# Down products of the feed-forward part on the full array as one sum, the turned tile in halves, and new orders inside the periods

## The reference, cut

```python
xn = layernorm(x)
# attention: 16 heads of width 16, 2 groups of keys and values
q = rotate(xn @ wq + bq);  k = rotate(xn @ wk + bk);  v = xn @ wv + bv
attn = softmax(q @ k.T * scale)            # (4, 16, 1024, 1024)
a = (attn @ v) @ wo + bo
# feed-forward part, 1024 hidden units
hidden = silu(xn @ W1.T) * (xn @ W3.T)
f = fwht(hidden) @ W2.T                    # fwht: Walsh-Hadamard along the hidden axis
out = x + a + f
```

## Time and profile before

| | |
|---|---|
| Median of 3 runs | 1179.03 us (1177.75 to 1181.44) |
| The profiled execution | 1181.6 us, span of instructions 1179.8 us |
| TensorE | 1049.8 us busy (89%), mean granted clock 0.936 |
| VectorE | 783.2 us (66%), of it 619.3 in 512 reductions of the units |
| ScalarE | 704.7 us (60%), of it 552.9 in 1024 exponentials |
| GpSimd | 352.2 us (30%) |
| Down products (L1352) | 1536 matmuls of 64 rows by 256 columns, 279 ns each on average |
| Additions of the down products (L1104, L1106) | 32 x 0.42 us and 32 x 0.42 us |
| Turned tiles (L896, L1089) | 7 casts of 1.01 us and 7 remainders of 1.22 us in `xt` |

### The profile page before, as it was taken

One profiled execution on the slowest core, in us unless ns is written; L12 is line 12 of the kernel. 1 busy time (PEld: TensorE's weight loads), 2 busy tenths in 40 slices (PEclk: granted clock), 3 DMA queues, 4 the chain that ended last, 5 costly groups with the idle time before them and its releaser, 6 DMA issues.

```text
span 1179.8 us, 19333 instructions
## 1 busy us (share of the span) xinstructions
PE 1049.8 (89%) x7584; PEld 547.5 (46%) x7584; DVE 783.2 (66%) x891; ACT 704.7 (60%) x1318; POOL 352.2 (30%) x299
## 2 busy tenths in 40 slices
PE   0358899989998999989998999989999999999994
PEld 0314354544555455544555445554445344544552
DVE  4895477757776577766777577765777777687611
ACT  2204377656765477655775567754775667656771
POOL 1652523107330254106330164204440023102310
PEclk9755799989999899989999799989999999999997
DMA  8247022412314223412205123421204101410001
GB/s 222 67 150 192 21 67 68 101 59 72 89 31 88 70 82 88 94 63 75 83 13 109 54 99 89 88 69 31 73 20 101 48 24 46 95 36 6 7 17 51
DMA packets 62732, 84.27 MB, mean 71 GB/s; under 512 B 16688, under 2 KB 31920, under 8 KB 62640
## 3 DMA queue, kind: packets, MB, share of 16 engines
q1 hardware_dynamic: 59328, 78.30, 24.8%
q10 hardware_dynamic: 3312, 4.72, 1.6%
HBM read 55.18 MB, written 22.54 MB: 66 GB/s over the span
## 4 chain that ended last, share of the span: by engine, by line
PE 79%; DVE 12%; ACT 3%; issue 2%; ACTq 1%; SPq 1%; DMA 1%; POOL 0%; POOLq 0%; DVEq 0%
PE ps L1387 19%; PE ps L1339 16%; PE ps L1374 15%; PE ps L1297 13%; DVE negpart L1124 9%; PE ps L1352 7%; PE ps L1277 3%; PE ps L1307 3%; ACT work L942 2%; PE ps L1313 1%; ACTq L878 1%; DVE y L1106 1%; PE ps L1302 0%; DVE y L1104 0%; ACT osum L950 0%
## 5 line engine op out<-in xcount | busy, mean ns | idle before, releaser
L1124 DVE TENSOR_REDUCE negpart<-ps 128x2 f32<-128x1024 f32 x512 | 619.3, 1223 | 272.6 <-PE ps L1297 267.7
L942 ACT ACTIVATE work<-ps 128x512 f32<-128x512 f32 x1024 | 552.9, 605 | 266.4 <-PE ps L1374 211.0
L1297 PE MATMUL ps<-kb,qh 48*128 48x512 f32 x1024 | 257.7, 472 | 53.4 <-DVE negpart L1124 27.4
L1374 PE MATMUL ps<-qh,kb 50*128 50x512 f32 x1024 | 272.0, 470 | 20.0 <-ACT work L942 19.3
L1387 PE MATMUL ps<-work,vb 128*32 128x512 f32 x2048 | 282.0, 626 | 0.0
L1374 PEld LDWEIGHTS ps<-qh,kb 50*128 50x128 f32 x1024 | 121.2, 192 | 218.9 <-ACT work L942 166.8
L1339 PE MATMUL ps<-xf,w_p 64*128 64x512 f32 x1536 | 207.1, 401 | 5.9 <-DVE negpart L1124 3.5
L1297 PEld LDWEIGHTS ps<-kb,qh 48*128 48x128 f32 x1024 | 109.2, 197 | 149.0 <-DVE negpart L1124 83.2
L1339 PEld LDWEIGHTS ps<-xf,w_p 64*128 64x128 f32 x1536 | 140.7, 186 | 52.6 <-DVE hid L1096 12.7
L825 POOL TENSOR_TENSOR hid_p<-hid,hid_p 128x512 fp32r<-128x512 f32 x64 | 82.3, 1286 | 196.0 <-ACT hid_p L933 196.0
L831 POOL TENSOR_TENSOR attnt<-attnt,recips 128x512 f32<-128x512 f32 x16 | 20.4, 1278 | 374.6 <-DMA recips<-recip_rows 374.6
(11 more groups left out here) (109 smaller groups left out, 489.0 us busy)
## 6 DMA issues: line engine op xcount, KB each, us to landing
xf<-xn_parts SPq DMA_DIRECT2D x32, 512.0 KB, 7.8
qh<-qk_parts SPq DMA_DIRECT2D x192, 64.0 KB, 2.2
xn_parts<-xt SPq DMA_DIRECT2D x14, 512.0 KB, 3.6
y<-in_x SPq DMA_DIRECT2D x8, 512.0 KB, 4.1
attnt<-osum SPq DMA_DIRECT2D x128, 32.0 KB, 2.0
recips<-recip_rows SPq DMA_DIRECT2D x128, 32.0 KB, 1.8
out<-y SPq DMA_DIRECT2D x8, 512.0 KB, 2.9
xn<-in_x SPq DMA_DIRECT2D x7, 512.0 KB, 4.5
```

The costliest lines, as they stand in the source:

```text
L942: nc.scalar.activation(prob[j % 2][:, h, :], ps[:, 4 + u % 3, :], ACT.Exp, scale=SCALE).then_inc(exp_done, 1)
L1124: nc.vector.tensor_reduce(negpart[a][:, f, :, h, t, e], two(slot), AX.X, ALU.max, negate=True).then_inc(ring_free[slot], 1)
L1297: m = pe.matmul(bank[:, r, :], qh[2 * q + f][rows, h, t * P:(t + 1) * P], kb[i % 2][rows, e * 512:(e + 1) * 512], start=True, stop=True)
L1374: pe.matmul(ps[:, 4 + u % 3, :], kb[i % 2][rows, kt * P:(kt + 1) * P], qh[2 * a + f][rows, h, :], start=True, stop=True).then_inc(s2_done, 1)
```

## The change

1. The down product is one matmul of 128 rows for each chunk and term instead of two of 64, all in bank 0 of its slot. `down` is one addition, and the semaphore `down_half` is gone.
2. The turned tile is handed over in halves: XT counts two fills and two frees, `turned_hi` and `turned_lo` take one half (128x512) each and are called twice.
3. The sequences of all three engines have new orders for most kinds: XT, QK, WO, WOx, DN, DNx, UPx for TensorE; on ScalarE gate stands before hidden_before in UP, projected(i + 2, 1) two exponentials later in QK, and hidden_before and save_finished move in others; on VectorE DN takes four units before `down` instead of three.

```diff
-FULLS = {"QK": 2}
-FREES = {"UP": 2, "VT": 2}
+FULLS = {"XT": 2, "QK": 2}
+FREES = {"XT": 2, "UP": 2, "VT": 2}
...
@@ -147,70 +147,67 @@
             first(1)
             sums_before()
             scores(1)
-            own(0)
-            first(1)
-            own(1)
+            extra()
+            own(0, 1)
+            first(1)
             scores(2)
             own(2)
-            first(1)
-            extra()
             scores(3)
+            first(1)
             own(3)
             sums(i, 2 * p)
         elif kind == "WO":
+            extra()
+            first(0)
+            first(0)
+            sums_before()
+            first(1)
             scores(0)
-            first(1)
+            scores(1)
+            own(0, 1, 2, 3)
+            scores(2)
+            sums(i, 2 * p)
+            first(1)
+            scores(3)
+        elif kind == "W2":
+            scores(0)
+            first(1)
+            sums_before()
+            scores(1)
+            first(1)
+            own(0, 1)
+            scores(2)
+            scores(3)
+            first(1)
+            sums(i, 2 * p)
             extra()
+            first(0)
+        elif kind == "XT":
+            first(1)
+            own(0, 1)
+            scores(0)
+            scores(1)
+            sums_before()
+            extra()
+            first(0)
+            first(1)
+            scores(2)
+            scores(3)
+            first(0)
+            sums(i, 2 * p)
+        elif kind == "QK":
+            scores(0)
+            first(1)
             first(0)
             scores(1)
             sums_before()
             scores(2)
-            sums(i, 2 * p)
-            own(0, 1)
-            first(1)
             scores(3)
-            own(2, 3)
-            first(1)
-        elif kind == "W2":
-            scores(0)
-            first(1)
-            sums_before()
-            scores(1)
-            first(1)
-            own(0, 1)
-            scores(2)
-            scores(3)
+            first(1)
+            own(0, 1, 2, 3)
             first(1)
             sums(i, 2 * p)
             extra()
-            first(0)
-        elif kind == "XT":
-            sums_before()
-            own(0)
-            first(1)
-            extra()
-            first(1)
-            scores(0)
-            own(1)
-            scores(1)
-            first(1)
-            scores(2)
-            first(0)
-            scores(3)
-            sums(i, 2 * p)
-        elif kind == "QK":
-            scores(0)
-            first(1)
-            first(0)
-            scores(1)
-            scores(2)
-            first(1)
-            sums_before()
-            own(0, 1, 2, 3)
-            first(1)
-            scores(3)
-            extra()
-            sums(i, 2 * p)
         elif kind is None:
             scores(0)
             first(0)
@@ -224,43 +221,43 @@
             scores(3)
             first(1)
         elif kind == "UPx":
+            scores(0)
             first(0)
-            scores(0)
+            first(1)
             sums_before()
             scores(1)
-            first(1)
-            own(0, 1)
-            first(1)
-            own(2, 3)
-            first(1)
+            own(0)
             scores(2)
+            first(1)
+            own(1, 2)
+            first(1)
+            own(3)
             sums(i, 2 * p)
             extra()
             scores(3)
         elif kind == "DNx":
+            sums_before()
+            first(1)
             scores(0)
+            own(0)
             scores(1)
+            first(1)
+            own(1, 2)
+            first(1)
+            own(3)
+            scores(2)
             first(0)
-            sums_before()
-            first(1)
-            own(0, 1)
-            scores(2)
-            own(2)
-            first(1)
-            own(3)
             scores(3)
+            extra()
             sums(i, 2 * p)
-            first(0)
-            extra()
         elif kind == "WOx":
             scores(0)
             first(1)
             own(0)
             scores(1)
-            own(1)
-            first(1)
             scores(2)
-            own(2, 3)
+            first(1)
+            own(1, 2, 3)
             first(1)
             sums_before()
             first(0)
...
@@ -887,13 +883,13 @@
                                              bias=nmr[:, t:t + 1], scale=rstd[:, t:t + 1])
                 a.then_inc(xn_done, 1)
 
-            def turned_hi(m):
+            def turned_hi(m, k):
                 slot = RING[("XT", m)][0]
-                act.wait_ge(*filled(("XT", m)))
-                if m > 1:
+                act.wait_ge(*filled(("XT", m), k + 1))
+                if m > 1 and k == 0:
                     act.wait_ge(*spilled(m - 1 if m > 2 else 0))
                     act.wait_ge(*filled(("Q2", m - 1 if m > 2 else 0)))
-                nc.scalar.copy(turned_x(m)[0][:, :, :], two(slot)).then_inc(xnt_hi, 1)
+                nc.scalar.copy(turned_x(m)[0][:, k, :], two(slot)[:, k, :]).then_inc(xnt_hi, 1)
 
...
@@ -997,28 +995,31 @@
                         exponentials(i, j, 0, 1)
                         save_finished(i, p)
                         exponentials(i, j, 1, 4)
+                        gate(i, p - 4)
                         hidden_before(i, p)
-                        gate(i, p - 4)
                         exponentials(i, j, 4, 5)
                         linear(i, p - 4)
                         exponentials(i, j, 5, 8)
                     elif kind == "DN":
-                        exponentials(i, j, 0, 1)
-                        save_finished(i, p)
-                        exponentials(i, j, 1, 2)
-                        hidden_before(i, p)
-                        exponentials(i, j, 2, 8)
-                    elif kind == "XT":
-                        turned_hi(i + 2)
-                        save_finished(i, p)
-                        exponentials(i, j, 0, 8)
-                    elif kind == "QK":
                         exponentials(i, j, 0, 4)
                         save_finished(i, p)
-                        exponentials(i, j, 4, 5)
+                        hidden_before(i, p)
+                        exponentials(i, j, 4, 8)
+                    elif kind == "XT":
+                        turned_hi(i + 2, 0)
+                        exponentials(i, j, 0, 1)
+                        turned_hi(i + 2, 1)
+                        exponentials(i, j, 1, 3)
+                        save_finished(i, p)
+                        exponentials(i, j, 3, 8)
+                    elif kind == "QK":
+                        exponentials(i, j, 0, 3)
+                        save_finished(i, p)
+                        exponentials(i, j, 3, 5)
                         projected(i + 2, 0)
+                        exponentials(i, j, 5, 7)
                         projected(i + 2, 1)
-                        exponentials(i, j, 5, 8)
+                        exponentials(i, j, 7, 8)
                         projected(i + 2, 2)
                     elif kind == "W2":
                         exponentials(i, j, 0, 2)
...
@@ -1083,10 +1081,10 @@
                     tile_stats(m, t)
                 block_stats(m)
 
-            def turned_lo(m):
+            def turned_lo(m, k):
                 slot = RING[("XT", m)][0]
-                dve.wait_ge(xnt_hi, m + 1)
-                nc.vector.tensor_tensor(turned_x(m)[1][:, :, :], two(slot), turned_x(m)[0][:, :, :].bitcast(F32),
+                dve.wait_ge(xnt_hi, DC * m + k + 1)
+                nc.vector.tensor_tensor(turned_x(m)[1][:, k, :], two(slot)[:, k, :], turned_x(m)[0][:, k, :].bitcast(F32),
                                         ALU.subtract).then_inc(ring_free[slot], 1)
 
             def gated(m, c):
@@ -1101,9 +1099,7 @@
                 if t == 0:
                     dve.wait_ge(ybase_done, m + 1)
                 at = y[:, m % 4, t, :]
-                nc.vector.tensor_tensor(at, at, two(slot)[:, 0, 0:D], ALU.add).then_inc(down_half, 1)
-                dve.wait_ge(down_half, BT * m + t + 1)
-                nc.vector.tensor_tensor(at, at, two(slot)[:, 1, 0:D], ALU.add).then_inc(ring_free[slot], 1)
+                nc.vector.tensor_tensor(at, at, two(slot)[:, 0, 0:D], ALU.add).then_inc(ring_free[slot], 1)
 
             def values(m):
                 slot = RING[("VT", m)][0]
...
@@ -1214,38 +1212,40 @@
                         units(i, u + 3, 1)
                     elif kind == "DN":
                         extra_before(i, p)
-                        units(i, u, 3)
+                        units(i, u, 4)
                         down(i, p - 12)
-                        units(i, u + 3, 1)
                     elif kind == "WO":
+                        units(i, u, 1)
                         extra_before(i, p)
-                        units(i, u, 3)
+                        units(i, u + 1, 1)
                         projected_sums(i - 1, p - 2)
-                        units(i, u + 3, 1)
```

(23 more changed lines are left out.)

43 lines of the change are left out of this document (22 added, 21 removed).

## The result

The changed kernel takes 1184.83 us (median of 12 runs, 1181.83 to 1190.3) against 1180.66 for the kernel before (12 runs, 1177.75 to 1183.16). The ratio is 1.004, 95% interval 1.0022 to 1.0057: slower by 0.4%, where 1165 was forecast.

The account below looks back on a forecast made before the run. It took PE's own step lengths plus the XT and QK periods as the bound. XT and QK -34, DN -4, last turn +4, first DN +5, UP and UPx +10.5, WO +5 gave -13.5: 1165 us, range 1146 to 1185.

Parts of the forecast that it names:

- XT and QK: Turned tile in halves and new orders: XT 7.5 us for 11.3, QK 10.2 for 12.3, clock staying up; -34 us.
- turn 0: In XT and QK: this turn reaches XT at the lower clock anyway, so 2 us less is saved, -34 not -36.
- The DN products and orders: DN and DNx: shape changes add 32 us of PE work, new orders remove 36 us of waits; -4 outside the last turn.
- rival (c): DN products: 128-row weight loads cannot run under 128-row matmuls, 0.10 us more each; +77 us, 1242; chance 0.02.
- the first DN period: First DN period of each turn: scores(0) waits 1.2 us for exponential 6 instead of about 0.4; 8 x 0.65 = +5.
- the last turn: DN periods of the last turn: PE has few units left to wait for, so shape changes stay unpaid; +4 us.
- Rival (b): DN periods: shape changes not absorbed, booked 36 us of waits stay; 1183 at half, 1201 with all; chance 0.16.
- UP, UPx and the first DN period: hidden_hi behind gate on ScalarE delays exponentials: UP +5, UPx +5.5, first DN period of a turn +5 us.
- the 7.8: Sign in UP periods: expected 7.6 us; over 7.8 would make the prediction wrong.
- WO: WO periods: one excursion less (-0.39), but scores(2) behind scores(1) waits 0.9 for exponentials 0 to 2; 12 x 0.4 = +5.
- Rival (a): XT and QK: PE's work too thin, clock still falls in each of six turns; +15 us, 1180, no change; chance 0.14.
- the three bounds: Bounds of the forecast's own range 1153 to 1176: DN stream, XT of 7 to 8.5 us, ScalarE's order costing 8 to 24.

Follow-up runs that it names:

- e7_old_wo_up: Changed kernel with the WO, WOx, UP and UPx orders of before; turned tile, DN and DNx as changed: 1160.65 us, ratio 0.9847 to the kernel before.
- e8_dn_part: Kernel before with the DN part alone: down products on the full array as one sum, new DN and DNx orders: 1190.23 us, ratio 1.0088.
- e6: Changed kernel with down products in 64-row pairs and two additions, and WO, WOx, UP and UPx orders of before: 1147.81 us, ratio 0.9736 to the kernel before.
- e4_wo_old: Changed kernel with the WO and WOx orders of the kernel before: 1165.89 us, ratio 0.9888 to the kernel before.
- e11_wo_only: Kernel before with the new WO and WOx orders alone: 1199.78 us, ratio 1.0168.
- e1_dn64: Changed kernel with all its orders, but down products in 64-row pairs and two additions: 1174.07 us, ratio 0.9945 to the kernel before.
- e3: Kernel before with the turned tile in halves and the new XT and QK orders alone: 1160.36 us, ratio 0.9856.
- e9: e7_old_wo_up with own(2, 3) as one run in DN and three reductions before down, not four: 1162.79 us, ratio 0.9858 to the kernel before.
- e10: e6 with the DNx orders of the kernel before too: 1156.85 us, ratio 0.9804 to the kernel before.
- e5_up_old: Changed kernel with gate again behind the casts of the hidden chunk on ScalarE in UP: 1183.71 us, ratio 1.0031 to the kernel before.
- e2: Kernel before with down products on the full array and one addition, no order changed: 1214.58 us, ratio 1.0285.

## Why the prediction was wrong

**XT and QK: right.** XT was laid out at 7.5 us and takes 7.50, with the clock up. QK is 10.46 for 10.2. The six turns give 30.8 of the 34: the five turns 1 to 5 save 3.85 us each in XT, as booked, turn 0 saves 0.6 (11.56 to 10.96, at the lower level) where 2 was booked, and QK is 0.26 longer than laid out, six times. The timeline after has the laid-out chain; the two waits were booked at 0.6 and 1.1 and come out at 0.46 and, in two pieces, 0.8 (the prediction's "no wait of PE is then over 0.8" doesn't fit its own 1.1; by the trace it holds):

```profile
505.24 0.50 PE L1297 MATMUL ps<-kb,qh 48*128 48x512 f32 x2
...
505.67 1.09 PE L1313 MATMUL ps<-ident,xn 128*128 128x128 f32 x8
...
507.88 0.50 PE L1373 MATMUL ps<-qh,kb 50*128 50x512 f32 x1 [0.46 <-ACT work L938]
...
510.58 0.99 PE L1373 MATMUL ps<-qh,kb 50*128 50x512 f32 x2 [0.31 <-ACT work L938]
```

**The DN products and orders: right in the sum, not in its parts.** Period 13 of turn 3, after:

```profile
614.08 0.49 PE L1373 MATMUL ps<-qh,kb 50*128 50x512 f32 x2
614.50 1.69 PE L1351 MATMUL ps<-w2t_p,hid_p 128*128 128x256 f32 x12
616.12 0.51 PE L1297 MATMUL ps<-kb,qh 48*128 48x512 f32 x2
616.47 0.40 PE L1373 MATMUL ps<-qh,kb 50*128 50x512 f32 x2
616.80 0.98 PE L1351 MATMUL ps<-w2t_p,hid_p 128*128 128x256 f32 x6
617.71 0.50 PE L1373 MATMUL ps<-qh,kb 50*128 50x512 f32 x2
```

From a score to the down matmul's stream 0.42 us pass (0.41 forecast), own(0, 1) with the way back takes 1.62 (1.58), own(2) 0.91 (0.89), the unit and score between 0.68 (0.64). A full-array matmul of 256 columns stands 0.115 to 0.12 from the next (0.22 behind the first of a piece), the load inside it, so rival (c) falls: what the Trainium skill (TensorE: Matmul & The Clock Gate, Part 3: Packing small matmuls) says in its list of what overlaps, that a load does so only where the row group differs, is not borne out for 128-row matmuls here; the same section's remark that a load can also go to a background weight buffer would fit. The period is 8.00 for 7.9. The excess is its first 0.90 us, laid out at 0.67. DNx is 8.99 (8.65 forecast), the first DN period 8.61 (8.89), the last 8.08 (7.95), and the last turn costs 4.0 (+4). In sum +6.2 for +5, but part of that is luck. The periods behind the first give back 1 us, not 4. The first DN period is longer for another reason than the one booked, ScalarE's order in UP: with that order as before it is longer still (8.88 in e7_old_wo_up, 8.85 in e8_dn_part), so its growth comes with the new products and orders of DN, and the sum had left it out there. And in the last turn e7 and e8 cost 2.4, not 4; the other 1.5 stand in its first DN period (9.09 us with the new UP order, 7.59 with the old), where the clock falls. Rival (b), the unpaid changes of shape, falls by its own sign, since a DN group is 33.6 us and not 36; but by the medians the DN part alone does cost 11 us (e8). What the forecast didn't ask is whether the orders need the full array at all. They don't: e6 against e7 puts the full array at a loss of 13 us.

**UP, UPx and the first DN period: half the size.** The three terms were +5, +5.5 and +5. The periods run from first instruction to first instruction, so a wait at the head of one lies in the row of the one before; they are read together: UP +6.3, UPx -0.6, and the first DN period at 8.61, where e7_old_wo_up, with the same DN order and UP as before, has 8.88. Against e7 that is about 7 us for 15.5. The UP periods ahead of UPx and DN are 0.3 longer each, 7.87 us and so over the 7.8 that the prediction named as a sign of being wrong; the others aren't longer. gate and the cast stand back to back ahead of the exponentials, as foreseen, but scores(0) at the head of UPx waits 0.24 us for its exponential and its second bank 0.48 more (0.98 for 0.50): 0.7 where 1.2 was booked.

```profile
553.28 0.60 ACT L917 ACTIVATE hid<-ps 128x512 f32<-128x512 f32 x1 [0.55 <-PE ps L1340]
...
553.78 0.61 ACT L929 CAST hid_p<-hid 128x512 fp32r<-128x512 f32 x1
...
555.91 0.98 PE L1373 MATMUL ps<-qh,kb 50*128 50x512 f32 x2 [0.24 <-ACT work L938]
```

**WO: the step that failed.** It was "scores(2) directly behind scores(1) waits 0.9 for exponentials 0 to 2: 12 x 0.4 = +5". For the ten WOx periods of turns 1 to 5 the size is about right: against e4_wo_old the new order costs 0.47 and 0.55 us a period without a fall, 5.1 in all. Another 0.9 us of the ledger's row comes from the first WOx period being 0.17 longer behind the new QK, with either WO order. What the term lacked is the rest. First, the clock: in turns 2 and 5 it falls in the second WOx period (+3.0 and +1.6), in turn 6 in the WO period (+1.5) and in turn 7 in the first WOx period (+2.5), 8.6 us in all that the sum had at nothing. Second, turns 6 and 7 without their falls: the two WO periods, which the 12 leaves out, cost 1.1 us each through the two neighbouring first(0) and the waits behind, and the two WOx periods 0.7 each, 3.7 in all. Together 18.3 for 5. Rival (a) had the mechanism, that PE's work gets too thin and the clock falls, with a chance of 0.14 and a price of 2.6 us a turn; but it looked for it in XT and QK alone, where it is now gone, and not where the change adds waits. e4_wo_old (-19) and e11_wo_only (+20) show the size from both sides.

**From the sum to the median.** The profiled executions differ by 0.6 us, the medians by 4.2. The profile after is near the lower end of its runs; the others scatter upwards by 8.5 us, where e4, e6 and e7 scatter by 4 to 6. More falls of the clock fit that: the mean granted clock is 0.953 in the four shortest of the twelve runs (1181.8 to 1184.1 us) and 0.946 in the two longest (1190.0 and 1190.3). In which periods those falls stand, no run shows, since one execution was profiled; and e1_dn64, with the same WO orders, scatters by 2.2 in five runs.

The time thus stands just inside the range given, at its slow end, with the sign of the less likely side. That range is narrower than its parts in one place: the three bounds named for the forecast's own range add up to 1150 to 1184, not 1153 to 1176.

## What to carry to other kernels

When a change adds waits to a stretch in which the engine already waits, price a fall of the clock beside the wait itself, at least as a rival: a second wait of 0.45 us in 3.3 brought no fall in three turns and one of 1.6 to 3 us in two. The order inside one period can bring a wait at its border with the next (e3, e9, e10): cost two periods together, and change the order before and behind in one step. And when an edit comes with a new order that pays for it, ask what the order brings without the edit: here 13 us more. Last, count the periods that a term covers: two WO periods with an order of their own were in no term.

## What the runs showed of the hardware

The clock falls in some turns and not in others with the same instructions: at 2.40 us busy of 3.30 in turn 2 it fell, at 2.41 in turn 3 it didn't. In e11_wo_only, with the same WO orders, it fell in each of turns 1 to 5, in e5_up_old in four of them, in e1_dn64 in turns 1 and 5. What decides between them stays open. In e4_wo_old, e6_and_dn64 and e7_old_wo_up, with the WO orders of before and the XT order of the change, no fall stands from turn 1 to the end of turn 6. The old orders are no safeguard, though: in the first WOx period of turn 7 the clock falls in e2, e8 and e10 (11.78, 10.28 and 11.78 us for 8.82), and not in the kernel before, e4, e6 and e7, with the same order.

A change of the array's shape costs about 0.2 us into the full array and about 0.2 back, in WO products before and in fp32r down products after alike. The Trainium skill (TensorEngine Tiling, Key Properties) says that changing the mode drains the engine, without a price; the rows fit that and put a price to it. And for fp32r at 256 columns, a 128-row matmul and a pair of 64-row ones both cost 0.115 to 0.12 us a step, so halving the count of matmuls gave no PE time at all.
